# A memset on GpSimd behind each embedding gather of a recommendation tower

## What is computed

```
e = stack([tbl_f[ids[:, f]] for f in range(50)], axis=1)      # 512 x 50 x 16
gram = einsum('bid,bjd->bij', e, e)
z = gram[:, I, J]                                             # pairs i < j, 1225 of them
h = concatenate([z, dense_ctx], axis=1)                       # 512 x 1241
h = maximum(h @ W_top1 + b_top1, 0)                           # 512
h = maximum(h @ W_top2 + b_top2, 0)                           # 256
y = h @ W_top3                                                # 1
```

## Time and profile before

| what | value |
|---|---|
| median of three runs | 265.6 us |
| the profiled execution's own time | 265.52 us |
| its span (first to last instruction) | 263.7 us |
| TensorE busy with matmuls | 129.4 us (49%) |
| VectorE busy | 97.4 us (37%) |
| ScalarE busy | 43.3 us (16%) |
| GpSimd busy | 92.9 us (35%) |
| gathers | 96 |

### The profile page before, as it was taken

One profiled execution on the slowest core, in us unless ns is written; L12 is line 12 of the kernel. 1 busy time (PEld: TensorE's weight loads), 2 busy tenths in 40 slices (PEclk: granted clock), 3 DMA queues, 4 the chain that ended last, 5 costly groups with the idle time before them and its releaser, 6 DMA issues.

```text
span 263.7 us, 2940 instructions
## 1 busy us (share of the span) xinstructions
PE 129.4 (49%) x1211; PEld 118.5 (45%) x1211; DVE 97.4 (37%) x166; ACT 43.3 (16%) x72; POOL 92.9 (35%) x100
## 2 busy tenths in 40 slices
PE   0384202200202210010119969992999935797795
PEld 0383101200202200000019969992998925787793
DVE  5384110200911001010006999449577572404201
ACT  8400000100030000000001513205105013135210
POOL 4777777777777777777000000000000000000000
PEclk9997555555555555555556988999599995599999
DMA  2999400000130000000000000000000000000000
GB/s 67 340 433 366 145 6 8 6 8 6 14 129 10 6 6 7 7 6 6 1 0 0 2 0 2 0 2 0 0 2 4 0 1 2 0 0 2 0 5 0
DMA packets 5648, 10.57 MB, mean 40 GB/s; under 512 B 2149, under 2 KB 4582, under 8 KB 5504
## 3 DMA queue, kind: packets, MB, share of 16 engines
q1 hardware_dynamic: 2562, 9.58, 9.9%
q0 software_dynamic: 3072, 0.79, 3.0%
HBM read 10.34 MB, written 0.03 MB: 39 GB/s over the span
## 4 chain that ended last, share of the span: by engine, by line
PE 34%; issue 22%; another core or an unknown queue 19%; DVE 16%; ACT 5%; DMA 2%; SPq 0%; DVEq 0%; ACTq 0%
PE p L594 10%; PE psm L553 7%; PE gram L568 5%; DVE picked L398 5%; PE gram L587 4%; DVE scols L428 3%; ACT blocks L174 2%; PE psm L594 2%; PE pt L649 2%; DVE fixed L387 2%; DMA wide<-quotients 2%; DVE onehot L412 1%; DVE z L180 1%; DVE mcols L447 1%
## 5 line engine op out<-in xcount | busy, mean ns | idle before, releaser
L553 PE MATMUL psm<-table,onehot 128*128 128x160 f32 x208 | 45.1, 372 | 67.7 <-DVE picked L398 30.1
L553 PEld LDWEIGHTS psm<-table,onehot 128*128 128x128 f32 x208 | 38.9, 243 | 71.0 <-issue 38.5
L398 DVE TENSOR_TENSOR picked<-psm,mask 128x480 f32<-128x480 f32 (+1 forms) x36 | 22.9, 637 | 92.5 <-remote 80.0
L241 POOL DMA_INDIRECT moving<-tbl,ids_sb x48 | 47.0, 979 | 16.9 <-issue 14.3
L246 POOL DMA_INDIRECT moving<-tbl,ids_sb x48 | 45.7, 952 | 14.6 <-issue 14.6
L594 PE MATMUL p<-z,w_sb 128*128 128x128 f32 x312 | 44.4, 294 | 1.6 <-DVE z L185 1.6
L594 PEld LDWEIGHTS p<-z,w_sb 128*128 128x128 f32 x312 | 41.7, 210 | 2.6 <-ACT z L185 1.8
L568 PE MATMUL gram<-blocks,scols 128*63 128x48 f32 x256 | 14.2, 238 | 47.1 <-issue 46.0
L568 PEld LDWEIGHTS gram<-blocks,scols 128*63 128x63 f32 x256 | 12.4, 155 | 49.4 <-issue 49.3
L180 DVE COPY z<-gram 63x384 f32<-63x384 f32 (+2 forms) x18 | 9.3, 516 | 44.2 <-PE gram L568 27.2
L387 DVE TENSOR_REDUCE fixed<-picked 128x48 f32<-128x480 f32 (+1 forms) x36 | 22.8, 635 | 1.2
(11 more groups left out here) (41 smaller groups left out, 55.2 us busy)
## 6 DMA issues: line engine op xcount, KB each, us to landing
wide<-quotients SPq DMA_DIRECT2D x4, 832.0 KB
w_sb<-in_w SPq DMA_DIRECT2D x1, 3072.0 KB
moving<-tbl,ids_sb POOLq DMA_INDIRECT x96
table<-in_small SPq DMA_DIRECT2D x1, 720.0 KB
table<-in_small SPq DMA_DIRECT2D x1, 640.0 KB
w_sb<-in_w SPq DMA_DIRECT2D x1, 512.0 KB
table<-in_small SPq DMA_DIRECT2D x1, 480.0 KB
table<-in_small SPq DMA_DIRECT2D x1, 240.0 KB, 2.6
```

The costliest lines, as they stand in the source:

```text
L241: nc.gpsimd.indirect_dma_start(moving[:, t, YS + n, 0:D], None, tables[n], bass.IndirectOffsetOnAxis(ap=ids_sb[:, t, NS + n:NS + n + 1], a ...
L398: nc.vector.tensor_tensor(picked[:, m % 3, 0:k], psm[:, m % 2, 0:k * R * D].rearrange("p (f r d) -> p f d r", r=R, d=D), mask[:, t, a:b, : ...
L553: ins = nc.tensor.matmul(psm[:, m % 2, (f - a) * R * D:(f - a + 1) * R * D], onehot[:, t % 2, f, :], table[:, f, :], start=True, stop=True)
```

## The change

A tile spacer of 128 partitions x 128 words is added, which nothing else uses, and a semaphore, spaced. Behind every gather GpSimd clears the whole of spacer; from the second gather on it first waits for the memset before. At the end it waits for all 96. The gathers, their order and their semaphores are the same.

```diff
+        spacer = sb("spacer", [P, P])
...
+        spaced = sem("spaced")
...
         @block.gpsimd
         def _(pool):
 
+            ticks = [0]
+
+            def gather(t, slot, table, field, landed):
+
+                nc.gpsimd.indirect_dma_start(
+                    moving[:, t, slot, 0:D], None, table,
+                    bass.IndirectOffsetOnAxis(ap=ids_sb[:, t, field:field + 1], axis=0),
+                ).then_inc(landed, 16)
+                if ticks[0]:
+                    pool.wait_ge(spaced, ticks[0])
+                nc.gpsimd.memset(spacer[:], 0.0).then_inc(spaced, 1)
+                ticks[0] += 1
+
             pool.wait_ge(ids_loaded, 16)
             for t in range(TILES):
                 for n in range(HALF):
-                    nc.gpsimd.indirect_dma_start(
-                        moving[:, t, YS + n, 0:D], None, tables[n],
-                        bass.IndirectOffsetOnAxis(ap=ids_sb[:, t, NS + n:NS + n + 1], axis=0),
-                    ).then_inc(mid_gathered[t], 16)
+                    gather(t, YS + n, tables[n], NS + n, mid_gathered[t])
                 for n in range(HALF):
-                    nc.gpsimd.indirect_dma_start(
-                        moving[:, t, XS + n, 0:D], None, tables[HALF + n],
-                        bass.IndirectOffsetOnAxis(ap=ids_sb[:, t, NS + HALF + n:NS + HALF + n + 1], axis=0),
-                    ).then_inc(tail_gathered if t == TILES - 1 and XS + n >= CUT else late_gathered[t], 16)
+                    gather(t, XS + n, tables[HALF + n], NS + HALF + n,
+                           tail_gathered if t == TILES - 1 and XS + n >= CUT else late_gathered[t])
+            pool.wait_ge(spaced, TILES * NL)
```

## The result

The changed kernel took 254.93 us in the median (254.34 to 260.02, four executions); the kernel before 265.45 us (263.01 to 265.6, four executions). The ratio is 0.9615, 95% interval 0.9556 to 0.9673: faster by 3.8%, where 178 us, faster by 33%, was forecast, with a range of 160 to 267 us. The profiled execution of the changed kernel is the one of 260.02 us, span 257.1; the other profiled spans lie at 251.6 to 253.2 us. What I read from its trace explains 6.6 us of span, and the other executions are some 5 us shorter still; where those 5 us come from was not looked at.

A forecast was written before the change was run, and what follows sets the result against it. TensorE was held to be slow for 138.5 us because gathers, sent faster than 1.40 us of service each, delayed its completions. Spaced gathers gave a 166 us floor, plus 10 us of waits, plus 1.8 outside the span: 178 us, range 160 to 267.

The forecast's parts named there:

- What bounds the kernel: Whole span: 138.5 us in which TensorE gets little done, its completions reported late, then 125.2 us of nearly dense work.
- The memset: GpSimd, behind each gather: adds 0.25 us (bounds 0 and 0.51), so the gather period becomes 1.50 us.
- there is no growing backlog, and TensorE should run as it does after 138.5 us: TensorE's slow stretch: at 1.50 us a gather against 1.40 us of service it vanishes and arrivals set the pace.
- The floor: End of span: the largest of three gather arrivals plus the old trace's remaining work, 166 us.
- the 10 us: Added to the 166 us for TensorE's waits at product_y and product_x and for half clock: 10 us.
- The backlog: Path shared with TensorE's completions: each gather leaves 1.40 us of work, sent every 1.25 us, so the queue never empties.
- Rival 3: Nothing happens: memset hides in the gap or costs under 0.15 us; TensorE free at 138.4 us, time 265.5 us; chance 0.12.
- Rival 1: Only part of the backlog is the gathers', SP's loads lay the rest; span 236 to 252, about 245 us; chance 0.20.
- Rival 2: TensorE crawls while gathers are in flight, however densely; dense piece 23.75 us later, time 289.3 us; chance 0.20.
- The wait: GpSimd, for the memset before: long met, nothing counted beyond the gap; the final wait is hidden by TensorE work.
- The port: Memset and VectorE writing SBUF side by side: taken as 0, at most 20 us, most beside idle time.

The follow-up runs named there:

- e8: Kernel before plus 1500 long-met waits on SP behind the last wide load; 263.88 us beside 265.36 us for the kernel before, ratio 0.997.
- e5: The changed kernel measured again, unaltered, in a set where the kernel before took 163.04 us; 162.69 us, ratio 0.989.
- e14: Changed kernel with a spacer of 288 words instead of 128; 193.5 and 198.37 us, beside 264.49 us for the kernel before.
- e2: Changed kernel with a spacer of 256 words instead of 128; 169.06 us beside 163.1 us for the kernel before, ratio 1.037.
- e3: Changed kernel with memsets going round seven spacer pieces, each waiting for the memset seven before; 163.43 us beside 163.1 us for the kernel before.
- e7: Kernel before plus 40 SP loads, each one 8-byte piece per partition; 162.49 us beside 163.28 us for the kernel before.
- e1: Changed kernel with a spacer of 512 words instead of 128; 188.09 us beside 163.1 us for the kernel before, ratio 1.159.
- e6: Kernel before plus 40 SP loads, each 8 single 4-byte words per partition; 162.02 us beside 163.28 us for the kernel before.

## Why the prediction was wrong

**What bounds the kernel** was read rightly, as far as the trace before could tell: a slow piece and a dense one of 125 us, and the slow piece was TensorE's completions being reported late. e8 adds that SP is held back there too, and e5 that the piece is absent without the condition.

**The memset** is the step that failed first: "I take 0.25 us, near the bare memset [...] The gather period becomes 1.50 us". The memset's 0.21 us was right (0.22), but what it adds between undisturbed gathers is 0.09 us, since nearly half of the old 0.30 us gap went into it; I had bounded the cost by this gap hiding the whole memset or staying whole, and not asked how much of it would be left. The period became 1.34 us, under the 1.40 us that the prediction had set as the limit, and the slow stretch stayed: 14.44 us of matmuls from 41 to 125 us, and a time of 254.93 us instead of 178. The mean over all gathers is 1.41 us, about at the limit, so by the mean the prediction's rule does not decide the case; by the undisturbed period it says what happened. A period like the forecast one (e14, 1.47 us undisturbed, mean 1.54) took the time to 196 us.

**"[...] there is no growing backlog, and TensorE should run as it does after 138.5 us"** is the second fault. Even at about the period that I had assumed, e14 took 196 us, not 178, with 37.6 us of waits that the profile cannot name, and the sum had no term for them. The floor for its last gather is 149.5 + 2.1 + 14.6 = 166 us as before, and its span of 191.0 us lies 25 us above it where I had allowed 10. Without the condition e2's span of 167.1 us lies 3 us above its own floor (147.7 + 2.1 + 14.6 = 164.4 us), so there the 10 us were too many. The reading that a path 91% full (1.40 / 1.54) still makes TensorE wait is an inference.

**The backlog** stands in its direction only. e14 shows that a longer memset, which spaces the gathers, takes most of the slow stretch away. Between the changed kernel and e14 the undisturbed period differs by 0.13 us and the time by 59 us. TensorE's recovery fits a service of 1.40 us a gather at the mean periods of 1.27 us, where it comes 14.7 us behind the start of the last gather, and of 1.41 us, where it comes 2.4 us behind. But the prediction had 1.40 us twice, for a gather's service and for a TensorE instruction, and took them as the same. The second fell to 0.68 us on average when the period rose by 0.14 us, so it is not a constant. And a queue of gathers alone is too short: by the prediction's numbers, the 30 gathers sent by 41.1 us in the kernel before leave 4 + 30 x 1.40 - 41.1 = 5 us of work, while a report came 25 us late; in the changed kernel the 58 sent by 82.4 us leave 3 us, and the report came 47 us late. So it is not only gathers that wait on that path; that TensorE's own reports, leaving slowly one by one, make up most of it is the likelier reading, and not tested. The direct test, half of the gathers, never met the condition. And the condition itself is not explained: without it 1.27 us is no load that can be seen.

**The rivals.** Rival 3 had the right condition (the memset costs less than 0.15 us, the stretch ends near 138.4 us; it ended near 140) and missed the time with 265.5 us: it took the slow piece as unchanged. In it TensorE got a report every 0.68 us on average instead of 1.40, and 10.5 us were gained in all. Rival 1 gave 245 us, nearer to the time by a hair, but by a wrong way: the stretch did not end at 107 to 125 us. (Its upper span should read 125 + 129 = 254 us, not 252.) Rival 2, the slower one, is excluded by the result and by e14. That the change could depend on something outside the program was not among the rivals, and it is the larger part of the truth: 101 us against 10.

**The wait** cost nothing that can be seen without the condition (e3). **The port** was taken at 0, and that is not quite so: VectorE was busy for 97.0 us without memsets (e7), 98.2 with memsets of 128 words (e5) and 105.6 with 512 words (e1), and its 32x384 copies took 519, 594 and 806 ns. In the changed kernel it came to nothing, with 97.3 us against 97.4.

## What to carry to other kernels

When an added instruction follows one that leaves a gap, ask what is left of the gap behind it; where a rate is held against a limit 12% away, half a gap can decide. Being just above such a limit did not mean running freely (e14): price the waits there too. An experiment that adds instructions has to be checked for when they ran: those of e8 nearly all ran behind the stretch that they were meant to load. And take the kernel before along in every measurement: here it alone showed that the same program takes 163 or 265 us, and that the change is worth 4% in one case and nothing in the other.

## What the runs showed of the hardware

- TensorE's completions can be held back by 25 us and more (a selection over at 41.1 us, its pick at 66.41 us) while single instructions of VectorE and GpSimd keep their length (a pick 0.66 us, a gather 0.94 us). With the condition this goes with the spacing of GpSimd's gathers: 1.40 us per TensorE instruction at a mean gather period of 1.27 us, 0.68 us on average at 1.41, and stalls of at most 8.7 us at 1.54.
- SP is held back in the same stretch: 39 of its long-met waits were recorded in 49 us, and 710 in the 45 us after the release at 138.0 us (e8).
- Where the condition is absent it is not brought about by transfers on SP's queue (41,600 packets in loads issued over 51 us, e6). What the condition consists of is open.
- A candidate by a page alone: the Trainium skill, NOTIFIC — the notification-queue block, section 7.1, says that the internal pipeline of the block that carries the records of instruction tracing always holds back its sources rather than lose a record, and that a nonzero stall counter would mean that this path had throttled an engine. No run here reads that counter and none of the twelve sets has an execution without tracing, so nothing shows that this is what happened, and nothing excludes that the slow stretch comes from the tracing.
- GpSimd: a memset begins as soon as a gather ends, and 0.17 us pass before the next gather, against 0.30 us between two gathers. A 128-word memset took 0.22 us, a 288-word one 0.36 us.
- VectorE's copies last longer beside longer memsets of GpSimd: 519 ns without (e7), 594 ns with 128 words (e5), 806 ns with 512 words (e1), for a pair product's 32x384 layout copy.
